# A macaron block (MoE, attention, MoE) on one core: the order of side work in the last attention batches, of the combines, and of the tail

## The reference, cut to what matters

```python
def ffn(x):                                   # x: (2048, 256)
    scores = sigmoid(x @ gate_w)              # 16 experts
    _, selected = top_k(scores + expert_bias, 2)
    w = scores[selected] / (sum of both + 1e-20)
    shared = silu(x @ shared_gate) * (x @ shared_up) @ shared_down
    routed = sum over the two experts e: w[e] * (silu(x @ gate_e) * (x @ up_e)) @ down_e
    return shared + routed

x = x + 0.5 * ffn(layernorm(x))
x = x + attention(layernorm(x))               # 3 heads of 256, softmax over the queries, mean of heads, fc
x = x + 0.5 * ffn(layernorm(x))
```

## Time and profile before

| what | value |
| --- | --- |
| median of 3 runs | 512.28 us (509.96 to 513.18) |
| the profiled execution's own time | 512.53 us |
| its span, first to last instruction | 511.3 us |
| TensorE clock granted, mean over the span | 0.956 of full |
| PE busy | 442.7 us, 87% |
| DVE busy | 342.4 us, 67% |
| ACT busy | 265.7 us, 52% |
| POOL busy | 278.3 us, 54% |

### The profile page before, as it was taken

The page is one execution under the profiler, slowest core; times in us unless marked ns, Lnnn a source line. Parts: engine busy times, 40 slices in busy tenths (PEclk is TensorE's granted clock), DMA queues, the critical chain, the costliest instruction groups (busy, mean ns, idle before and its releaser), DMA issues. The chain is left out here.

```text
span 511.3 us, 10128 instructions
## 1 busy us (share of the span) xinstructions
PE 442.7 (87%) x2951; PEld 394.0 (77%) x2951; DVE 342.4 (67%) x1053; ACT 265.7 (52%) x708; POOL 278.3 (54%) x322
## 2 busy tenths in 40 slices
PE   1676799999787899999999999989979888999982
PEld 1345699899666789988889888979868677899972
DVE  6589575565448575458646875675685786777778
ACT  4855376676523455543544454435434663577750
POOL 5267875565064643386344746738657167266660
PEclk9977699999989999999999999999998988999995
DMA  8672375576632100011000111104001466366968
GB/s 295 242 226 92 114 210 160 189 207 130 160 94 63 53 21 1 1 52 35 28 12 22 53 31 50 57 3 141 31 33 62 153 222 213 102 189 188 303 227 254
DMA packets 44468, 60.33 MB, mean 118 GB/s; under 512 B 6080, under 2 KB 36800, under 8 KB 44416
## 3 DMA queue, kind: packets, MB, share of 16 engines
q1 hardware_dynamic: 34688, 37.11, 23.2%
q0 software_dynamic: 7584, 20.98, 13.7%
q10 hardware_dynamic: 2144, 1.60, 1.0%
HBM read 34.75 MB, written 24.91 MB: 117 GB/s over the span
## 5 line engine op out<-in xcount | busy, mean ns | idle before, releaser
L2099 POOL TENSOR_TENSOR e_sp<-raw,e_sp 128x512 fp32r<-128x512 f32 x48 | 62.2, 1296 | 69.5 <-ACT e_sp L1163 69.0
L400 PE MATMUL bank<-v_sp,e_sp 128*128 128x256 f32 x576 | 78.1, 286 | 2.4 <-DVE x_sb L1703 2.0
L400 PEld LDWEIGHTS bank<-v_sp,e_sp 128*128 128x128 f32 x576 | 75.4, 193 | 6.2 <-issue 2.8
L400 PE MATMUL bank<-g_sp,xT 128*128 128x512 f32 x288 | 75.5, 398 | 0.1
L2063 POOL DMA_INDIRECT raw<-xn_dram,gather_at x47 | 45.6, 971 | 30.9 <-PE bank L406 27.1
L2025 POOL DMA_INDIRECT pair_dram<-raw,slot_i x47 | 45.8, 974 | 30.1 <-ACT raw L1055 26.7
L1186 ACT ACTIVATE raw<-bank,softmax_row 128x512 f32<-128x512 f32 x48 | 33.2, 691 | 55.1 <-DVE softmax_row L1854 54.7
L400 PEld LDWEIGHTS bank<-g_sp,xT 128*128 128x128 f32 x288 | 52.0, 190 | 9.5 <-issue 0.2
L400 PE MATMUL bank<-w_hi,e_sp 128*128 x188 | 51.6, 297 | 1.2 <-DVE e_sp L1672 1.1
L1854 DVE TENSOR_REDUCE softmax_row<-bank 128x1 f32<-128x512 f32 x48 | 32.9, 686 | 25.8 <-PE bank L400 25.3
L1672 DVE TENSOR_TENSOR e_sp<-bank,e_sp 128x128 fp32r<-128x128 f32 x94 | 27.2, 290 | 31.8 <-ACT e_sp L1025 31.1
(11 more groups left out here) (287 smaller groups left out, 1089.6 us busy)
## 6 DMA issues: line engine op xcount, KB each, us to landing
stage<-slab_dram SPq DMA_DIRECT2D x47, 136.0 KB
y_dram<-stage SPq DMA_DIRECT2D x47, 128.0 KB, 3.0
late_pair<-pair_dram SPq DMA_DIRECT2D x16, 256.0 KB, 4.3
slab_dram<-stage SPq DMA_DIRECT2D x17, 136.0 KB
stage<-in_w_pack SPq DMA_DIRECT2D x6, 384.0 KB, 4.9
stage_more<-in_w_pack SPq DMA_DIRECT2D x6, 384.0 KB, 3.2
x_sb<-in_x SPq DMA_DIRECT2D x4, 512.0 KB, 7.0
xn_dram<-xn_all SPq DMA_DIRECT2D x4, 512.0 KB, 5.2
```

What stands on the lines that cost most here:

```text
L400: m = pe.matmul(dst, lhs[k][l], rhs[k][r], start=(first and k == 0 and i == 0), stop=(last and k == n - 1 and i == 2), skip_group_check=True)
L2099: pool.tensor_tensor(e_sp[:, i, 1, :], e32[:, i, :], e_sp[:, i, 0, :].bitcast(F32), ALU.subtract).then_inc(s_e_lo, 1)
```

## The change

It has these parts.

- Attention, VectorE: in the second unit of batches 1, 2 and 3 the side piece stands behind the rest of the values, no longer ahead of `attn_out` (batches 1 and 2) or between `attn_out` and the reciprocal (batch 3).
- Attention, TensorE: the rank of batch 2 stands one piece later, the packing of the table two pieces later; VectorE's `write_table` one slot later, and one memset goes from the last batch to batch 1.
- Second FFN, first nine tiles: batch 2's shared expert is taken out of this stage, and runs behind the last tile, ahead of batch 3's. Batch 1's `shared_lo` stands one step earlier, and the next tiles no longer wait for batch 2's sinks.
- The pair loads of token tiles 0 to 7 are issued three tiles earlier.
- Combines: 12 of the 32 combine instructions stand in steps 37 to 50 of the loop, in every second step and at its end.
- The tail: both `shared_gu` follow on TensorE, the rest of the combines stands between the pieces of the two shared experts; SP stores token tiles 0 to 3, which ScalarE's queue did before.

```diff
+    COMBINES_AT = {37: 1, 39: 1, 41: 1, 43: 1, 45: 1, 47: 1, 48: 2, 49: 2, 50: 2}
...
         def shared_turned(r, b):
-            return late_hT if r == 1 and b % 2 == 0 else shared_hT
+            return shared_hT if r == 0 or b % 2 else late_hT if b == 0 else tail_hT
...
                 elif r == 1 and b == 2:
-                    pe.wait_ge(s_act, BASE[1] + FULL_TILES)
+                    pe.wait_ge(s_act, DONE[1])
...
-                            if again:
-                                pe.wait_ge(s_ssink, 2 * B + 5)
-                            elif r == 1:
+                            if r == 1 and not again:
                                 pe.wait_ge(s_g_lo, 2 * B * HEADS)
...
-                        if again and g == lo + 1:
-                            pe.wait_ge(s_ssink, 2 * B + 6)
...
                 yield from prev_front(b - 1)
-                for _ in range(2 if b < B - 1 else 3):
+                for _ in range(2 if b < B - 1 else 4):
                     yield
                 rank_again(b - 1)
                 yield
                 if b == B - 1:
-                    for _ in range(4):
+                    for _ in range(5):
                         yield
                     pack_table(False)
...
-                elif s == 10:
-                    shared_gu(1, 2)
...
-            def open_late(s):
-                if s == FULL_TILES:
-                    shared_y(1, 2, (1,))
-
             shared_y(1, 1)
-            shared_y(1, 2, (0,))
-            ffn(1, open_late, FULL_TILES)
+            ffn(1, lambda s: None, FULL_TILES)
+            shared_gu(1, 2)
             shared_gu(1, 3)
+            shared_y(1, 2)
             shared_y(1, 3)
...
+                turn_of_batch = b > 0 and u % PER_BATCH == 1
+                if b + 1 < B and not turn_of_batch:
                     side_pieces(u, b, attn_side, ffn_side)
                 if late is not None:
                     attn_out(late)
-                if b + 1 == B:
+                if b + 1 == B and not turn_of_batch:
                     side_pieces(u, b, attn_side, ffn_side)
...
+                if turn_of_batch:
+                    side_pieces(u, b, attn_side, ffn_side)
                 side_pieces_late(u, b, ffn_side)
...
+            combines = (step for t in range(0, 2 * TB, 2) for step in combine_two(t))
+
+            def combine_some(s):
+                for _ in range(COMBINES_AT.get(s, 0)):
+                    next(combines)
+
+            ffn(1, combine_some, FULL_TILES)
+            shared_mul(1, 2)
+            for _ in range(2):
+                next(combines)
             shared_lo(1, 2)
...
             shared_mul(1, 3)
-            for t in range(TB, 2 * TB, 2):
-                combine_two(t)
+            next(combines)
             shared_lo(1, 3)
+            run(combines)
+            shared_sink(1, 2)
             for t in range(2 * TB, LATE_T, 2):
-                combine_two(t)
+                run(combine_two(t))
             shared_sink(1, 3)
             for t in range(LATE_T, NT, 2):
-                combine_two(t)
+                run(combine_two(t))
...
                 if t == 0:
-                    sp.wait_ge(s_ssink, 2 * B + 6)
+                    sp.wait_ge(s_ssink, 2 * B + 4)
...
-            for t in range(len(PAIRS_AT), NT):
+            for t in range(len(PAIRS_AT), LATE_T):
+                load_pair(t)
+            for t in range(TB):
+                store(t)
+            for t in range(LATE_T, NT):
                 load_pair(t)
```

More of the change, by code:

```diff
@@ L74, in macaron @@
     CLASS_TILES = [max(FULL_TILES + E, (b + 1) * TB * TOPK + E - 1) for b in range(B - 1)] + [NI]
[L75 removed]
+    COMBINES_AT = {37: 1, 39: 1, 41: 1, 43: 1, 45: 1, 47: 1, 48: 2, 49: 2, 50: 2}
+    PAIRS_AT = {34: 0, 35: 1, 36: 2, 37: 3, 40: 4, 41: 5, 42: 6, 43: 7}
     TILES = (NI, NI)
@@ L299, in shared_banks @@
             if r == 1:
-                return ((7, 5), (1, 0), (3, 2), (0, 1))[b]
+                return ((7, 5), (1, 0), (2, 3), (0, 1))[b]
             if b >= EARLY_SHARED:
@@ L305, in shared_turned @@
         def shared_turned(r, b):
-            return late_hT if r == 1 and b % 2 == 0 else shared_hT
+            return shared_hT if r == 0 or b % 2 else late_hT if b == 0 else tail_hT
         def shared_gated(r, b):
-            return late_h if r == 1 and b % 2 == 0 else shared_h[0 if r == 1 else b % 2]
+            return shared_h[b % 2 if r == 0 else 0] if r == 0 or b % 2 else late_h if b == 0 else tail_h
         def shared_y_banks(r, b):
@@ L1205, in act_program @@
             shared_hi(1, 1)
+            ffn(1, lambda s: None, FULL_TILES)
+            shared_silu(1, 2)
+            shared_silu(1, 3)
             shared_hi(1, 2)
-            ffn(1, lambda s: None, FULL_TILES)
-            shared_silu(1, 3)
             shared_hi(1, 3)
-            for q in range(LATE_T):
+            for q in range(TB, LATE_T):
                 act.wait_ge(s_comb, combined(q))
@@ L1591, in combine_two @@
                                                  op1=ALU.add).then_inc(s_comb, 1)
+                        yield
             def first_combine(t):
@@ L1725, in previous_front @@
                 count_class(b - 1)
+                if b == 1:
+                    chained(dve.memset(full_cap[:], float(FULL_TILES * P)))
                 yield
                 if b == B - 1:
-                    chained(dve.memset(full_cap[:], float(FULL_TILES * P)))
                     chained(dve.memset(list_first[:, LISTED:], 2.0 * E * SLAB))
@@ L1737, in previous_front @@
                     yield
-                    write_table(False)
                     next(rest)
                     yield
+                    write_table(False)
                     next(rest)
@@ L1886, in dve_program @@
             ffn(1, between2, 0, FULL_TILES, late_score_front)
-            shared_lo(1, 2)
-            shared_sink(1, 1)
-            def open_late(s):
-                if s == FULL_TILES:
-                    shared_sink(1, 2, (0,))
-            def open_mid(s):
-                if s == FULL_TILES + 1:
-                    shared_sink(1, 2, (1,))
-            ffn(1, open_late, FULL_TILES, mid=open_mid)
-            for t in range(0, TB, 2):
-                combine_two(t)
+            shared_sink(1, 1)
+            combines = (step for t in range(0, 2 * TB, 2) for step in combine_two(t))
[6 more added lines that the diff above has]
+                next(combines)
+            shared_lo(1, 2)
             shared_mul(1, 3)
-            for t in range(TB, 2 * TB, 2):
-                combine_two(t)
+            next(combines)
             shared_lo(1, 3)
+            run(combines)
+            shared_sink(1, 2)
             for t in range(2 * TB, LATE_T, 2):
-                combine_two(t)
+                run(combine_two(t))
             shared_sink(1, 3)
             for t in range(LATE_T, NT, 2):
-                combine_two(t)
+                run(combine_two(t))
         def pool_program():
@@ L2237, in tail2, with store @@
                 for q in range(LATE_T, NT):
-                    sp.wait_ge(s_comb, combined(q))
-                    sp.dma_start(out_rows[q], x_sb[:, q, :]).then_inc(s_out, 16)
+                    store(q)
                     yield
+            def store(q):
+                sp.wait_ge(s_comb, combined(q))
+                sp.dma_start(out_rows[q], x_sb[:, q, :]).then_inc(s_out, 16)
             load_x(0)
```

10 lines of the change are left out of this document (3 added, 7 removed).

## The result

The changed kernel takes 516.87 us in the median of 13 runs (514.33 to 520.69); the kernel before took 512.28 beside it. The ratio is 1.0093 (95% interval 1.0069 to 1.0118): slower by nearly 1%, where 510.8 us, a little faster, was forecast, and outside the range that ended at 515. The profiled execution took 515.20 with a span of 514.0, so it is one of the quicker ones: it shows 2.7 of the 4.6 us between the medians. What follows explains these 2.7; that the other 1.9 have the same causes is likely and not shown.

The account below looks back on a forecast made before the run. PE was taken to bound attention and the loop, so only its stalls could be won, and DVE the tail. Attention -1.85, seam -2.3, loop +0.2 and tail +2.2 gave -1.75 from 512.53: 510.8 us, range 504.5 to 515.0.

Parts of the forecast that it names:

- Batches 1 and 2: Attention: PE's two waits for `attn_out` at a new batch's first mix go, DVE's cost being covered; -2.0 us.
- Case E: Loop: a combine and a GpSimd scatter exclude each other at shared SBUF ports, up to 5.8 us, 516.4 us; chance 0.06.
- +0.95: Attention, batch 3: the stall of 1.39 is exchanged for a longer PE pause at the first `raw` row; +0.95 us.
- +0.7 for the clock: Attention, batch 3: PE's clock may fall behind the new pause; middle of 0 and +1.5, +0.7 us.
- Rank -1.15: Attention: batch 2's rank, one piece later, no longer waits for `choice`, and its small matmuls leave the values' path; -1.15 us.
- table -0.35: Attention: packing the table two pieces later loses its 2.69 stall, but POOL sets the end, so only -0.35 us.
- The seam: Behind the nine first tiles: without batch 2's shared expert, the last loop's gate and up begin earlier; -2.3 us.
- the tail: After the last tile: fewer combines, but DVE idles ahead of batch 2's product and its `shared_lo`; +2.2 us.
- The loop: 38 tiles: combines mostly fit DVE's idle time, +0.2 us; row loads queued behind earlier pair loads cost 0.
- Rival D: Loop: combines make DVE's `xt_lo` late and stand on PE's path; 514.5 us, slower than before; chance 0.10.
- Case B: Whole kernel: all stalls are won, no pause or clock price in batch 3, tail even; 505.0 us; chance 0.22.

Follow-up runs that it names:

- x10: Changed kernel, with GpSimd's subtraction in the second unit of batches 1 and 2 waiting for VectorE's moved combine; attention 221.84 us, ratio 1.0058 to the kernel before.
- (d): Fourth instruction group of x4: twelve VectorE instructions with two SBUF operands beside one indirect DMA of GpSimd; at most 0.01 us longer each.
- x4: Kernel before plus four groups of twelve VectorE instructions on dead buffers beside GpSimd, one trace; beside combines of 0.48 us, a GpSimd subtraction took 4.60 instead of 1.26.
- x3: Changed kernel with the side piece moved in batch 3 alone, at its old place in batches 1 and 2; attention 221.93 us, ratio 1.0047 to the kernel before.
- x1: Changed kernel with the side piece of batches 1, 2 and 3 back at its old place; attention 219.54 us, ratio 1.002 to the kernel before.
- x5: Changed kernel with no combine in the loop, pair loads still three tiles earlier; ratio 1.0152 to the kernel before, four runs.
- x2: Changed kernel with the side piece moved in batches 1 and 2 alone, at its old place in batch 3; attention 220.82 us, ratio 1.0058 to the kernel before.
- x6: Changed kernel with pair loads at their old place and 11 combines in the loop, three steps later; ratio 1.0068 to the kernel before, run again 1.0055.
- x9: Kernel before with later rank and table slots, eleven combines in the loop, and `attn_out` ahead of the side piece in all batches; attention 223.51 us, ratio 1.0048.
- x8: Kernel before with rank, look-up table and `write_table` in later slots and nothing else; attention 219.55 us, ratio 0.9984.
- x11: Kernel before with later rank and table, eleven loop combines, batches 1 and 2's side piece behind the values, GpSimd's subtraction held until the combine is done; ratio 0.9941.

## Why the prediction was wrong, step by step

1. **Batches 1 and 2, forecast -2.0, came out +1.3.** The step that failed: "What it costs DVE there is covered: DVE works 33.15 of 50 us in such a stretch". That is a mean over 290 to 340, of which only the first 7 us hold combines of the side pieces (the last starts at 296.8). In the 20 us behind the first mix of batch 1 the trace of before already had DVE busy for 15.89:

```profile
222.00:242.00 20.00, 18.96 (x124) 16.93 (x123) 15.89 (x47) 9.13 (x21) 13.92 (x13) 1.00 0.15 46
```

   and 3.3 of the 4.1 idle are the 0.60 to 0.86 ahead of each `v_sp`, for ScalarE. So VectorE had little left to give; that no order takes these waits away is argued, not shown. x10 shows what the two waits were worth without most of the hold-up: 0.2 us. The other 1.5 is the hold-up of the combine.

2. **Case E had the right mechanism at the wrong neighbour.** The prediction weighed the rule of the shared ports against a scatter, saw a combine of 0.41 beside it, and gave the rule 0.06. (d) of x4 agrees: a DMA issue of GpSimd costs VectorE nothing. But the same rule was never asked of the combine that the change moves in attention, where GpSimd's neighbour is a subtraction with operands in SBUF.

3. **Batch 3, forecast +0.95 and +0.7 for the clock, came out +2.4** (x3 less x1). The pause came as worked out: VectorE's `raw` row at 345.44, PE idle for 2.29 (2.4 forecast). The term that was mis-sized is the +0.95. x5 has the same attention program and the same pause, and its clock stayed full:

```profile
349.06 0.44 PE L409 MATMUL bank<-ident,raw 128*128 128x128 f32 x2 [2.28 <-DVE raw L1243]
349.25 3.00 PE L403 MATMUL bank<-xT,a_sp 128*128 128x512 f32 x12
...
380.10 0.98 PE L403 MATMUL bank<-b_sp,xT 128*128 128x256 f32 x6 [1.86 <-DVE v_sp L1862]
```

```profile
349.00:353.00 4.00, 3.94 (x19) 3.29 (x20) 3.40 (x6) 2.14 (x5) 3.69 (x5) 1.00 0.11 39
```

   Its last mix lies at 222.67, 1.85 behind that of x2 (220.82), which has batch 3's piece at its old place. At unit 39 the difference is 0.84 (187.64 and 186.80), near the forecast; the other 1.0 comes at 380.10, where the values wait 1.86, and 0.86 in x2. The prediction saw that VectorE's row maximum and the other rows stand behind the waiting one, and gave that no price; that this is what makes the later values late is likely and not shown.
   The clock costs 1.5 at the place (4.39 against 2.91, and unit 39 at 189.17 against 187.64), but only 0.53 at the last mix (223.20 against 222.67), since the later wait shrinks from 1.86 to 0.85. The 0.7 was not far off. Whether the clock falls wasn't to be foreseen: seven traces have this pause, of 2.27 to 2.39. The clock fell around the pause's end (0.4 us ahead of it to 1.5 behind) in four (changed, x3, x6 again, x10) and not in c0 (the changed kernel again), x5 and x6; in c0 and x6 it fell behind the next long pause, of 2.25 and 1.93. Of x9's two pauses the one of 2.15 had the fall and the one of 2.25 had not; the pause of 2.69 at the table had it, and its 2.68 in x4. So these traces don't tell by the length alone where it falls.

4. **Rank -1.15 and table -0.35 were right in sum:** -1.33 for the rank, and for the table -2.22, of which 2.12 came back by the last mix, which waits 1.0 for GpSimd's `e_sp` (0.4 before), as the step said. x8 has -1.30 for both.

5. **The seam, forecast -2.3, measured -2.56; the tail, forecast +2.2, measured +2.16.** The first idle place of the tail was forecast as 2.0 (2.01), the second as 1.1 (0.92). Both steps held, also inside: `e_sp` of tile 8 lies 0.99 closer to the last mix (0.93 forecast) and the down product of batch 1 1.11 closer (about 1.0).

6. **The loop, forecast +0.2, came out +1.58.** The step that failed: "a row load has some four tiles of advance, so I cost that at 0". The combines, which the step priced, cost nothing that can be read; the row loads, which it put at nothing, made PE wait 1.4. The longer wait, 0.97 for tile 38, has four pair loads of 256 KB right ahead of its row (466.35 to 470.18); PE had the row 6.3 us after its issue. Only the wait for tile 43, 0.43, lies behind the stop of 3.5 us in which the load of pair 4 waits for scatters that three tiles earlier are not out. How much of a row's delay is queueing on SP and how much the transfer, no run separates.

Rival D, the slower side, named the loop and the wrong cause in it: it asked 3.9 for combines, which cost nothing, and the late rows cost 1.4. Case B's sum takes 1.6 off for a tail that is "even instead of +2.2"; by its own words that is 2.2, and its time 504.4 instead of 505.0, which changes nothing here.

## What to carry to other kernels

Before a wait for a busy engine is counted as a gain, follow the releasing engine through the next few units at that place: where its only idle time is spent on hand-overs from others, the wait comes back at the next product that it makes. The same goes for a price: what one pause costs is read at the end of the stage, since a later wait can add to it or swallow it. A moved instruction is to be laid beside what the other engines do at the new place, GpSimd above all, and a moved load beside what queues behind it and what has to be done before it may go. Leaving the parts that pay (rank slots, combines in idle time of the loop) and dropping those that don't turned a kernel 0.9% slower into one 0.6% faster (x11).

## What was not expected of the hardware

- A run of VectorE instructions with two SBUF operands, back to back, kept a GpSimd subtraction of 1.26 us waiting for 3.3 us, while eight more of them began (x4, one trace); in the other order one instruction of VectorE took up to 2.00 instead of 0.48.
- Making GpSimd wait for a semaphore, 1.3 us, at a place where its result is needed 4 us later, made attention 1.36 us shorter (x10).
- The granted clock fell behind some pauses of 2.27 to 2.39 us and not behind others, in traces of the same program for attention (four of seven).
- The same kernel took 4.6% longer in two of the four rounds of experiments (534 to 536 us against 510 to 511), and it isn't the chip alone: the one that the record numbers 13 took 534.40 in one round and 510.88 in a later one. None of the loss is in attention or tail. In the loop PE waits 5.1 us in eight places for nothing that the profile shows (the changed kernel again, 402 to 520). Why is open.
